# Wide layers: output projections in half chunks in every step, scores and transposes issued alternately

## The reference, cut to what matters

```python
# wide layer (L0, L2): 16 heads of 64, column bias, output bias
q, k, v = x @ Wq, ctx @ Wk, ctx @ Wv
probs = softmax(q @ k.T * 64**-0.5 + col_bias)      # per head, 512 x 77
x = (probs @ v) @ Wo + bo + x
# narrow layer (L1, L3): rmsnorm, 16 query heads of 32, 4 key/value heads
q = rmsnorm(x, norm_w) @ wq
x = x + (softmax(q @ k.T / sqrt(32)) @ v) @ wo
```

## Time and profile before

| | us |
|---|---|
| median of 3 runs | 2069.18 (2068.88 to 2070.52) |
| the profiled execution | 2069.05 |
| its span | 2067.3 |
| PE busy | 2027.7 (98%) |
| PEld busy | 1762.3 (85%) |
| DVE busy | 1404.0 (68%) |
| ACT busy | 966.7 (47%) |
| POOL busy | 646.3 (31%) |

### The profile page before, as it was taken

One profiled execution on the slowest core, in us unless ns is written; L12 is line 12 of the kernel. 1 busy time (PEld: TensorE's weight loads), 2 busy tenths in 40 slices (PEclk: granted clock), 3 DMA queues, 4 the chain that ended last, 5 costly groups with the idle time before them and its releaser, 6 DMA issues.

```text
span 2067.3 us, 31200 instructions
## 1 busy us (share of the span) xinstructions
PE 2027.7 (98%) x11482; PEld 1762.3 (85%) x11482; DVE 1404.0 (68%) x2424; ACT 966.7 (47%) x1814; POOL 646.3 (31%) x518
## 2 busy tenths in 40 slices
PE   8999999999999998999999999999999989999998
PEld 8999988888888887788888888888888877888887
DVE  4432365775568556788888676557755675888886
ACT  3222263553445344555555454335433553555553
POOL 0000042322232254454443441223212533444441
PEclk9999999999999999999999999999999999999999
DMA  8688832222122222233333332212221232233322
GB/s 232 165 172 195 187 94 62 73 67 74 54 73 70 66 83 71 83 106 97 88 97 95 104 98 64 76 56 68 65 79 51 72 90 68 74 91 92 88 72 84
DMA packets 262537, 191.02 MB, mean 92 GB/s; under 512 B 197522, under 2 KB 199986, under 8 KB 259826
## 3 DMA queue, kind: packets, MB, share of 16 engines
q1 hardware_dynamic: 262386, 189.03, 34.8%
HBM read 132.66 MB, written 56.26 MB: 91 GB/s over the span
## 4 chain that ended last, share of the span: by engine, by line
PE 50%; issue 30%; POOL 11%; DVE 6%; ACT 1%; DMA 1%; SPq 0%; POOLq 0%; DVEq 0%; ACTq 0%
PE acc_bank L889 6%; POOL prob L1326 6%; PE t_bank L869 4%; PE acc_bank L261 4%; PE acc_bank L263 4%; PE acc_bank L262 4%; PE ctx_bank L261 4%; PE ctx_bank L262 4%; PE ctx_bank L263 4%; PE q_bank L847 4%; PE q_bank L849 3%; PE q_bank L851 3%; POOL x_s L1301 3%; PE s_bank L261 2%; POOL rest L1335 2%
## 5 line engine op out<-in xcount | busy, mean ns | idle before, releaser
L1326 POOL TENSOR_TENSOR prob<-prob,rinv 128x1232 f32<-128x1232 f32 x128 | 288.3, 2253 | 1011.4 <-DVE rinv L1207 1011.4
L1065 ACT ACTIVATE q_s<-q_bank 128x512 fp32r<-128x512 f32 x192 | 114.7, 597 | 491.6 <-PE q_bank L851 488.5
L889 PE MATMUL acc_bank<-pT_s,vals_s 128*128 128x512 f32 x1024 | 339.4, 417 | 0.0
L847 PE MATMUL q_bank<-x_s,w_s 128*128 128x512 f32 x768 | 319.9, 417 | 0.0
L849 PE MATMUL q_bank<-x_s,w_s 128*128 128x512 f32 x768 | 313.6, 408 | 0.0
L851 PE MATMUL q_bank<-x_s,w_s 128*128 128x512 f32 x768 | 313.0, 408 | 0.0
L1165 DVE TENSOR_REDUCE mx<-s_bank 128x4 f32<-128x308 f32 x512 | 239.9, 469 | 106.5 <-PE s_bank L813 54.1
L261 PE MATMUL acc_bank<-o_s,w_s 128*128 128x512 f32 x752 | 300.3, 399 | 0.2
L263 PE MATMUL acc_bank<-o_s,w_s 128*128 128x512 f32 x752 | 293.5, 390 | 0.0
L262 PE MATMUL acc_bank<-o_s,w_s 128*128 128x512 f32 x752 | 292.9, 390 | 0.0
L1056 ACT ACTIVATE prob<-prob,rstd 128x308 f32<-128x308 f32 x256 | 141.5, 553 | 265.5 <-DVE prob L1169 255.1
(11 more groups left out here) (107 smaller groups left out, 4095.0 us busy)
## 6 DMA issues: line engine op xcount, KB each, us to landing
stream<-x_back SPq DMA_DIRECT2D x128, 256.0 KB, 2.6
x_front<-stream SPq DMA_DIRECT2D x96, 256.0 KB, 3.3
x_back<-stream SPq DMA_DIRECT2D x96, 256.0 KB, 3.9
kvw_raw<-kvw SPq DMA_DIRECT2D x17, 1024.0 KB, 8.4
k_scr<-k_out SPq DMA_DIRECT2D x36, 308.0 KB, 8.8
keys_s<-k_scr SPq DMA_DIRECT2D x128, 77.0 KB, 2.5
v_scr<-v_out SPq DMA_DIRECT2D x8, 1024.0 KB
vals_s<-v_scr SPq DMA_DIRECT2D x512, 6.5 KB
```

What stands on the lines that cost most here:

```text
L847: pe.matmul(out, w[0], x_now[0], start=k == 0, stop=False)
L889: mm = pe.matmul(out, w, pT_s[:, part], start=i == mine[0] and part == 2 * n and w is v[0], stop=i == mine[-1] and w is terms[-1][0] and p ...
L1326: pool.tensor_tensor(view, view, rinv[:, slot].unsqueeze(2).broadcast_to([P, TILES * GH, CTX]), ALU.mult).then_inc(p_norm, 1)
```

## The change

A wide chunk is made in two halves h of 12 matmuls, each accumulated and added to x_back by itself (the bias with the first). The halves of batch gb stand two to a step in steps 4gb+4 to 4gb+7, so every wide step from the fifth on has two, and those of the last batch fill the first four narrow steps. The wide steps with a projection are called woven: their order on PE, ACT and DVE is written anew. Of the four score tiles the first stands among half of the queries, and each of the other three is issued alternately with one group of four transposes; values, half chunks and the other queries stand in blocks between these. In the first four narrow steps (`behind`) the first half chunk stands before score tiles 2 and 3, the second at the end. The quarters of wqB stand in two steps. DVE makes 128 additions of wide chunks in place of 64. The hunks below are from the plan, from PE (`woven`, the two branches) and, the last, from DVE.

```diff
-           ("wqB", 0, 0, (29, 29, 29, 29)), ("woB", 0, 1, (32, 33, 34, 35)),
+           ("wqB", 0, 0, (29, 29, 30, 30)), ("woB", 0, 1, (32, 33, 34, 35)),
...
-            projections = [("proj", gb, m) for gb, m in self.projections(s)]
-            if self.ahead(s):
-                acc += projections
-            if 0 <= s - 2 < NU:
-                acc += [("pv", s - 2, m) for m in range(kind(s - 2).Q)]
-            if not self.ahead(s):
-                acc += projections
+            projections = [("proj", *item) for item in self.projections(s)]
+            values = [("pv", s - 2, m) for m in range(kind(s - 2).Q)] if 0 <= s - 2 < NU else []
+            if self.woven(s):
+                acc += values[:1] + projections[:1] + values[1:] + projections[1:]
+            elif self.behind(s):
+                acc += projections[:1] + values + projections[1:]
+            else:
+                acc += values + projections
...
+            for h in range(kind(GROUPS * gb).halves):
+                for m in range(XC):
+                    if layer % 2 == 0:
+                        at = GROUPS * gb + 4 + 2 * h + m // 2
+                    else:
+                        at = GROUPS * gb + 5 + (m if b < B - 1 else m // 2)
...
+            def woven(small, turns):
+                for _ in range(6):
+                    next(small, None)
+                    next(turns, None)
...
+                elif plan.woven(s):
+                    beside(scores(s, 0), q, 12)
+                    run(v, 4 if kind(s - 2).name == "A" else 9)
+                    woven(scores(s, 1), turns(0))
+                    for item in projections[:1]:
+                        project(*item)
+                    run(v, 4)
+                    woven(scores(s, 2), turns(1))
+                    run(q, 12)
+                    woven(scores(s, 3), turns(2))
+                    for item in projections[1:]:
+                        project(*item)
...
                     run(q, half)
+                    if plan.behind(s):
+                        project(*projections.pop(0))
                     run(scores(s, 2), 1)
                     run(scores(s, 3), 1)
-                    if plan.ahead(s):
-                        for gb, m in plan.projections(s):
-                            project(gb, m)
...
+                if plan.woven(s):
+                    for item in plan.late(s - 1):
+                        add_result(*item)
+                    if s >= 2 and plan.rest_later(s - 2):
+                        rest_t(s - 2, TWICE)
+                    tile_scores(s, 0)
+                    next(q, None)
+                    if pv:
+                        rest_o(s - 2, 0)
+                    tile_scores(s, 1)
+                    turned(0)
+                    for item in projections[:1]:
+                        add_result(*item)
+                    if pv == 2:
+                        rest_o(s - 2, 1)
+                    tile_scores(s, 2)
+                    turned(1)
+                    next(q, None)
+                    tile_scores(s, 3)
+                    denominators(s)
+                    for item in projections[1:]:
+                        add_result(*item)
```

More of the change, by code:

```diff
@@ L149, in late, with woven, behind, whole @@
         found = self.projections(s) if s >= 0 else []
[L150 to L158, removed]
+        return found[-1:] if s < NU and kind(s).name == "B" else []
+    def woven(self, s):
+        return s < NU and kind(s).name == "A" and len(self.projections(s)) > 0
+    def behind(self, s):
+        return s < NU and kind(s).name == "B" and any(kind(GROUPS * gb).name == "A" for gb, _, _ in self.projections(s))
+    def whole(self, items):
+        return [(gb, m) for gb, m, h in items if h == kind(GROUPS * gb).halves - 1]
     def projections(self, s):
@@ L164, in projections @@
             layer, b = divmod(gb, B)
[L165 to L174, removed]
+            for h in range(kind(GROUPS * gb).halves):
[4 more added lines that the diff above has]
+                        at = GROUPS * gb + 5 + (m if b < B - 1 else m // 2)
+                    if at == s:
+                        found.append((gb, m, h))
         return found
@@ L233, in vals_zeroed, with weights_ready @@
         return 2 * (u // UNITS) + u % 2 + 1 if u % UNITS < 2 else 0
-    def weights_ready(self, what, layer):
-        names = {"q": ("wqA1", "wqB"), "o": ("woA1", "woB")}[what]
-        found = [n for n, piece in enumerate(PIECES) if piece[1] == layer // 2 and piece[0] == names[layer % 2]]
+    def weights_ready(self, name, layer):
+        found = [n for n, piece in enumerate(PIECES) if piece[1] == layer // 2 and piece[0] == name]
         return found[-1] + 1 if found else 0
@@ L784, in _ @@
                             load_weights(n + 2)
-                for gb, m in plan.projections(s):
-                    if (gb, m) not in plan.late(s):
-                        store(gb, m)
+                for gb, m in plan.whole([i for i in plan.projections(s) if i not in plan.late(s)]):
+                    store(gb, m)
             for m in range(XC):
@@ L830, in queries @@
                 if u % UNITS == 0:
-                    after(pe, w_lo, plan.weights_ready("q", u // UNITS))
+                    after(pe, w_lo, plan.weights_ready("wqA1" if kind(u).name == "A" else "wqB", u // UNITS))
                 for m in range(kind(u).Q):
@@ L1244, in _ @@
                         rest_t(s - 2, TWICE)
-                    for gb, m in plan.late(s - 1):
-                        add_result(gb, m)
-                    if not plan.early(s):
+                    for item in plan.late(s - 1):
+                        add_result(*item)
+                    if s >= 2:
                         next(q, None)
@@ L1270, in _ @@
                             tile_scores(s, t)
-                    for gb, m in plan.late(s - 1):
-                        add_result(gb, m)
-                    if plan.ahead(s):
+                    for item in plan.late(s - 1):
+                        add_result(*item)
+                    if plan.behind(s):
+                        add_result(*projections.pop(0))
                         denominators(s)
-                        for gb, m in plan.projections(s):
-                            add_result(gb, m)
-                    turned(0)
-                    if s < NU and not plan.ahead(s):
-                        denominators(s)
+                        turned(0)
+                    else:
+                        turned(0)
+                        if s < NU:
+                            denominators(s)
                     next(q, None)
@@ L1287, in _ @@
                     turned(2)
-                    for gb, m in plan.projections(s):
-                        if (gb, m) not in plan.late(s) and not plan.ahead(s):
-                            add_result(gb, m)
+                    for item in projections:
+                        if item not in plan.late(s):
+                            add_result(*item)
             for m in range(XC):
```

109 lines of the change are left out of this document (67 added, 42 removed).

## The result

| | before | after |
|---|---|---|
| median | 2069.35 (2068.88 to 2070.52) | 2051.45 (2049.6 to 2051.81) |
| ratio after/before | | 0.9911, 95% interval 0.9897 to 0.9924 |
| span of the profiled execution | 2067.3 | 2049.7 |

What follows compares the result with a forecast made beforehand. PE, busy for 98% of the span, was taken to bound the kernel; 2069.05 - 27 (woven steps) - 13 (turns) + 2 (single losses) = 2031 us, with an eight-in-ten range of 2016 to 2058.

Steps and rivals of the forecast that it cites:

- woven steps: Wide steps with projection, 59 of them: each 0.45 us shorter by alternating scores and transposes, 27 us in all.
- the two turns: Steps around the change to a narrow layer (31 to 37 the first): 6.4 us gained at each, 13 in all.
- once each: Single losses: first transposes wait in steps 4, 65 and 68, 4.6 us lost; 2.4 gained elsewhere; net 2 lost.
- the forecast's own lower bound of 21 us: Whole kernel: least gain within the forecast's own bounds, 59 x 0.3 + 7 - 4 = 21 us (2048).
- the new wait before the values: Steps 33 to 35, behind score tile 3: values wait for DVE's late half-chunk addition, 2.5 us each, 7.5 a turn.
- rival 4: Turns lose as much as before or more by the new bank wait, alternation gives little: 2065 to 2075; chance 0.03.
- rival 1: Woven steps: alternation gives nothing, every small matmul being held by a weight load of 0.11; time 2055 us; chance 0.13.
- The pair of score and transpose: Woven steps: one score matmul alternating with one transpose takes 0.185 us, with ends of 0.18 and 0.24.
- I take 0.075, nearest to the stream: Woven pair: time from score to transpose, chosen near the score's 0.07 us stream; alternatives 0.085 and 0.13.
- I let 2.1 more go to the clock: At each turn: 2.1 us allowed for clock falls beyond 11.6 us of waits, against 20.1 lost before.
- a gain of 7 at the turns and not 13: Both turns together: 7 us gained with as many clock falls as before; 13 forecast, 17 without any fall.
- a gain of 0.4 alone: Steps 29 and 93: splitting wqB over two steps ends a wait of 0.4 us at each.

Runs made afterwards that it cites:

- experiment 1: Changed kernel, but in woven steps a score tile's six matmuls stand before its four transposes instead of alternating: 2061.29 us, ratio 0.9962.
- Experiment 6: Changed kernel, but from the ninth unit of each wide layer on score matmuls stream 76 columns in place of 154: 2048.22 us, one run.
- experiment 7: Changed kernel, but from the ninth unit of each wide layer on transposes have only 64 columns of weights: 2044.46 us, one run.
- experiment 3: Changed kernel plus 9 unused 512-column matmuls right before the values in each of steps 33 to 35 and 97 to 99: 2042.17 us, ratio 0.9869.
- experiment 4: Changed kernel, but all four quarters of wqB stand in step 29 (93), as in the kernel before: 2064.23 us, ratio 0.9976.
- experiment 8: Transposes of 64 rows from each wide layer's ninth unit on, one run each: 2200.82 us in the changed kernel, 2074.81 in the one before.
- experiment 9: Changed kernel with, in the first four narrow steps, late half chunk added after score tile 1 and first transposes' rest before the sums: 2033.36 us, ratio 0.9826.

## Why the prediction was right or wrong

The spans differ by 17.6 us where 38 were forecast. By the steps: 57 woven steps x 0.3025 = 17.2 gained and the two turns (steps 31 to 37, 95 to 101) 2 x 2.1 = 4.2, against 3.2 lost once each and 0.7 in the first part; sum 17.5. The 0.7 is no work of the change: the first part took from 265.1 to 267.0 us in the profiles of this case. Against the forecast are missing 57 x 0.15 = 8.6 in the woven steps, 2 x 4.75 = 9.5 at the turns (6.4 and the 0.45 of weaving step 31, less 2.1), 1.2 once each and the 0.7: 20.0, and some 0.6 is rounding in the forecast's own sum. The gain also lies below the forecast's own lower bound of 21 us.

**The direction and the mechanism were right.** PE bounds the kernel; the alternation shortens each pair; the new wait before the values came where and as long as forecast (2.5 us in steps 33 to 35 and 97 to 99). No rival came true, though rival 4 was near in its first half: by the prediction's own prices a turn still loses some 18 us where it had lost 20.1. The rearranging without the alternation gives 0.04 a step (experiment 1), where 0.06 was worked out in rival 1.

**The pair of score and transpose was mis-sized.** "I take 0.075, nearest to the stream" was the choice that failed: with the prediction's 0.109 to 0.11 for the way from transpose to score, the pair of 0.196 leaves 0.085 to 0.087 from score to transpose, the value that the prediction itself had from the delay and the light load of the earlier trace rows. A delay that a row shows should have gone into the sum; the stream was only the lower bound. Experiment 6 shows that the score's stream alone does not set the pair, experiment 7 that the transpose's load has a part of some 0.01; that the rest is the delay agrees in size and is not shown, nor is the split of the pair in two parts. 12 pairs x 0.011 = 0.13 a step of the 0.15 missing; the rest is not traced.

**The turns were mis-sized by the clock.** Of "I let 2.1 more go to the clock" 4.8 came true: three falls at 1.6 (experiments 1 and 3). I took for granted that waits shorter than the 3.7 us of the earlier trace rows would mostly pass, and none of the six did. The trace before could have told: in steps 33 and 36 it has gaps of 2.17 and 2.74 us by starts, and a fall of the clock behind each (windows before):

```profile
799.20:802.60 3.40, 3.40 (x12) 2.71 (x11) 1.88 (x4) 1.70 (x3) 1.05 (x1) 0.50 0.31 94
850.40:853.80 3.40, 3.40 (x11) 2.93 (x12) 1.71 (x4) 1.75 (x4) 0.00 (x0) 0.50 0.31 81
```

With the one in step 32 these were three falls at a turn, the 5.0 us of the prediction, and there are three after: the case for which the prediction had a gain of 7 at the turns and not 13. The clock is 2.7 of the 4.75 that a turn misses.

**Steps 30 and 31 were left out.** Step 31 lost 1.2: it stops for the last quarters of wqB, which the split has moved next to their use, and once among its values, behind DVE's split of the transposed probabilities (PE, in brackets the idle time before, which overlapping records understate; by starts the gaps are 0.62 and 0.90):

```profile
758.65 0.50 PE L849 MATMUL q_bank<-x_s,w_s 128*128 128x512 f32 x1 [0.39 <-POOL w_s L1387]
763.43 0.50 PE L893 MATMUL acc_bank<-pT_s,vals_s 128*128 128x512 f32 x1 [0.50 <-DVE pT_s L1225]
```

In step 30, and in 94, two values start 0.72 apart where 0.23 are usual, and the step takes 0.6 more. I had counted the split of wqB as a gain of 0.4 alone. In experiment 4 step 31 takes 14.15 us and has neither stop, though there DVE had the longer step 30 to catch up in. Steps 36 and 37 lose 2.6 where I had 1.9, steps 33 to 35 some 0.3 more than three times 2.5 and the clock, step 32 1.9 for 2.2. With the clock and the 0.15 of weaving step 31 this is 2.7 + 1.2 + 0.7 + 0.3 - 0.3 + 0.15 = 4.75, what a turn misses. The excess in steps 4, 65 and 68 came to 1.83, 1.07 and 1.75 us, 4.65 in all, forecast 4.6; what the list of single losses lacked are the 2 x 0.6 of steps 30 and 94.

**What stays open.** What holds the pair at 0.186 once the transpose's load is short; no run shortens the transpose's stream alone. Why the clock fell after nearly every wait of 2.5 us, and not in steps 97 and 98 of experiments 1 and 6 nor in 33 and 97 of experiments 7 and 8, with the same gap of 2.57, nor after the gaps of 1.99 in experiment 9. Why DVE's split comes late in steps 30 and 31.

## What to carry to other kernels

Where two kinds of small matmuls alternate, put into the sum every delay that a row of weight loads shows, also where it lies hidden now, for the alternation may bare it. A wait of PE costs its length and possibly a stretch at 1.2 GHz behind it; count the falls in the trace before, with the wait ahead of each, price them per wait, and try filling it before removing it. When work is spread evenly over short steps, look at what a long step had hidden on the other engines (weights prepared on ACT and POOL), and place each bank's drain in the idle time of its engine rather than at the end of a block.

## What was not expected of the hardware

- A transpose of 64 rows between matmuls of 128 rows makes a pair of 0.47 us against 0.196, and no weight load starts ahead of its own matmul there (experiment 8).
- Waits of 2.5 us on PE were each followed by 3.4 us at 1.2 GHz in the changed kernel, some 1.6 us lost each time (in experiments 1, 6, 7 and 8 after four of the six); nine matmuls in each wait took all six falls away (experiment 3).
- Two different matmuls alternating are not held by the longer of stream and load alone: 0.196 a pair, where the streams make some 0.18, and halving the score's stream leaves it at 0.196 (experiment 6).
